# Splitting every transfer of rows on 125 partitions into one of 112 and one of 13 partitions

## The reference

```
x = x + graph_0(layernorm(x), edges, types64)   # attention of each edge's source, softmax by destination
x = x + experts_0(layernorm(x))                 # 2 of 8 experts per node
x = x + graph_1(layernorm(x), edges, types6)    # sums by relation, attention over 6 relations
x = x + experts_1(layernorm(x))                 # 2 of 8 experts, hidden size 1024
x = x + graph_2(layernorm(x), degree**-0.5)     # normalised neighbour sums, then a product
x = x + experts_2(layernorm(x))                 # dense over 8 experts
x = x + graph_3(layernorm(x), edges)            # neighbour sums
x = x + experts_3(layernorm(x))                 # shared and 4 gated experts
```

## Time and profile before

| | us |
|---|---|
| median of 3 runs | 4976.39 (4974.26 to 4980.61) |
| profiled execution, its time | 4979.84 |
| profiled execution, its span | 4977.6 |
| PE busy / DVE busy / ACT busy / POOL busy | 84% / 53% / 31% / 37% of the span |
| queue of SP's transfers: packets, MB | 405810, 490.95 |

### The profile page before, as it was taken

One profiled execution on the slowest core, in us unless ns is written; L12 is line 12 of the kernel. 1 busy time (PEld: TensorE's weight loads), 2 busy tenths in 40 slices (PEclk: granted clock), 3 DMA queues, 4 the chain that ended last, 5 costly groups with the idle time before them and its releaser, 6 DMA issues. The chain is left out here.

```text
span 4977.6 us, 70703 instructions
## 1 busy us (share of the span) xinstructions
PE 4160.5 (84%) x21605; PEld 3198.6 (64%) x21605; DVE 2661.7 (53%) x5828; ACT 1549.6 (31%) x3042; POOL 1840.2 (37%) x1628
## 2 busy tenths in 40 slices
PE   4899995864917999889999668997799999979978
PEld 2565653643715666568888657886687767768855
DVE  4588888888138999836665560002433322233354
ACT  0233331011314333345565324443001333310023
POOL 0477773872446767536666402113100000000011
PEclk9899997986968999999999879998899999999989
DMA  1599994830845666647666419996423000022200
GB/s 66 177 286 287 295 281 141 260 98 26 264 145 166 181 181 182 190 149 204 184 180 170 138 44 338 323 323 189 122 74 88 1 1 1 2 82 77 61 14 26
DMA packets 519774, 748.78 MB, mean 150 GB/s; under 512 B 80123, under 2 KB 438273, under 8 KB 519301
## 3 DMA queue, kind: packets, MB, share of 16 engines
q1 hardware_dynamic: 405810, 490.95, 31.9%
q0 software_dynamic: 62656, 189.33, 13.8%
q10 hardware_dynamic: 50960, 64.09, 3.7%
HBM read 526.98 MB, written 217.19 MB: 150 GB/s over the span
## 5 line engine op out<-in xcount | busy, mean ns | idle before, releaser
L2828 PE MATMUL sum_ps<-table_rows,block_weights 128*125 128x256 f32 x2500 | 564.7, 386 | 37.1 <-DMA table_rows<-k_table 37.1
L2828 PEld LDWEIGHTS sum_ps<-table_rows,block_weights 128*125 128x125 f32 x2500 | 465.6, 189 | 136.2 <-issue 70.2
L109 POOL DMA_INDIRECT rows_all<-kv_table,src_of_visit x416 | 445.1, 1070 | 221.6 <-issue 111.8
L2632 POOL TENSOR_TENSOR window_sums<-window_sums,brought_blocks 128x650 f32<-128x650 f32 x320 | 427.8, 1337 | 223.6 <-ACT running_blocks L2642 140.2
L2521 POOL DMA_INDIRECT gathered_rows<-k_table,src_of_chunk x392 | 409.2, 1044 | 208.4 <-issue 113.9
L2743 PE MATMUL sum_ps<-gathered_rows,hit 128*126 x1376 | 364.6, 390 | 22.6 <-DVE window_sums L2709 19.0
L2810 DVE TENSOR_TENSOR block_weights<-raw 128x625 f32<-128x625 uint16 x248 | 183.6, 805 | 349.7 <-PE sum_ps L2828 323.6
L2570 PE MATMUL block_ps<-cell_hot,low_hot 128*128 128x325 bf16 x1280 | 231.8, 304 | 141.5 <-DVE cell_hot L2560 140.4
L2057 DVE TENSOR_TENSOR y<-out_ps,b 128x256 f32<-128x256 f32 x120 | 51.0, 425 | 553.0 <-PE out_ps L1956 553.0
L3327 POOL MEMSET eps<- 125x1 f32 x1 | 0.1, 98 | 917.8 <-POOLq L2770 917.8
L2579 ACT ACTIVATE block_copies<-block_ps 128x650 bf16<-128x650 f32 x320 | 227.9, 712 | 358.1 <-PE block_ps L2570 356.7
(11 more groups left out here) (500 smaller groups left out, 8245.8 us busy)
## 6 DMA issues: line engine op xcount, KB each, us to landing
w<-in_L_ffn_W SPq DMA_DIRECT2D x112, 1024.0 KB, 7.5
v_kept<-rows_all SPq DMA_DIRECT2D x104, 512.0 KB, 5.0
v_rows<-v_kept SPq DMA_DIRECT2D x104, 512.0 KB, 4.5
visit_blocks<-block_copies ACTq DMA_DIRECT2D x320, 162.5 KB, 2.9
brought_blocks<-visit_blocks SPq DMA_DIRECT2D x320, 162.5 KB, 3.3
blocks<-running_blocks SPq DMA_DIRECT2D x320, 162.5 KB, 3.5
raw<-blocks SPq DMA_DIRECT2D x250, 162.5 KB, 2.2
w<-in_L_ffn_w SPq DMA_DIRECT2D x64, 256.0 KB, 3.7
```

The lines of the kernel that those rows point to most:

```text
L109: pool.indirect_dma_start(env.ring[:, k % KEPT_RING, i, :], None, env.kv_table, bass.IndirectOffsetOnAxis(env.src_of_visit[:, k * VB + i:k ...
L2632: pool.tensor_tensor(self.totals[:, k % 2, :], self.totals[:, (k - 1) % 2, :], self.brought[:, k % self.BROUGHT, :], ALU.add).then_inc(sel ...
L2828: mm = pe.matmul(sum_ps[0:P, t % banks, 0:D], weights[0:k, t % floats, h, :], rows[0:k, h, :], start=h == 0, stop=h == BH - 1)
```

## The change

Two constants are added: `HALVES = ((0, 112), (112, P))` and `BOTH = 16 * len(HALVES)`. At each of the eleven places where rows on 125 partitions are loaded or stored, the one transfer becomes a loop over `HALVES` with two transfers of the same bytes, one of partitions 0 to 111 and one of partitions 112 to 124, both on the same semaphore, and every wait that counted 16 for such a transfer counts 32. Broadcast loads on 125 partitions (biases, `gamma`, `beta`) stay as they are, and so do all transfers on 128 partitions. The diff, cut to its kinds:

```diff
+HALVES = ((0, 112), (112, P))
+BOTH = 16 * len(HALVES)
...
-                sp.dma_start(env.x[:], a["x"].rearrange("(t p) d -> p t d", p=P)).then_inc(x_landed, 16)
+                for lo, hi in HALVES:
+                    sp.dma_start(env.x[lo:hi], a["x"].rearrange("(t p) d -> p t d", p=P)[lo:hi]).then_inc(x_landed, 16)
...
-                sp.wait_ge(x_landed, 16)
+                sp.wait_ge(x_landed, BOTH)
...
-                    sp.dma_start(env.kv_table[g * GN:(g + 1) * GN, :].rearrange("(t p) d -> p t d", p=P),
-                                 kv_rows[:, half * GT:(half + 1) * GT, :]).then_inc(kv_stored[half], 16)
+                    for lo, hi in HALVES:
+                        sp.dma_start(env.kv_table[g * GN:(g + 1) * GN, :].rearrange("(t p) d -> p t d", p=P)[lo:hi],
+                                     kv_rows[lo:hi, half * GT:(half + 1) * GT, :]).then_inc(kv_stored[half], 16)
...
-                    pool.wait_ge(kv_stored[half], 16 * len(range(half, G, 2)))
+                    pool.wait_ge(kv_stored[half], BOTH * len(range(half, G, 2)))
...
-                        v.wait_ge(kv_stored[g % 2], 16 * (g // 2))
+                        v.wait_ge(kv_stored[g % 2], BOTH * (g // 2))
...
-                        sp.dma_start(env.rows[:, g * GT:(g + 1) * GT, :], env.kv_table[g * GN:(g + 1) * GN, D:2 * D].rearrange(
-                            "(t p) d -> p t d", p=P)).then_inc(own_landed, 16)
-                sp.wait_ge(own_landed, 16 * G)
+                        for lo, hi in HALVES:
+                            sp.dma_start(env.rows[lo:hi, g * GT:(g + 1) * GT, :], env.kv_table[g * GN:(g + 1) * GN, D:2 * D].rearrange(
+                                "(t p) d -> p t d", p=P)[lo:hi]).then_inc(own_landed, 16)
+                sp.wait_ge(own_landed, BOTH * G)
...
-                    sp.dma_start(env.x[:, ts, :], env.x_kept[:, ts, :]).then_inc(x_landed[g], 16)
-                    sp.dma_start(o_rows[:, ts, :], rows_of(env.o_table, g)).then_inc(o_landed[g], 16)
+                    for lo, hi in HALVES:
+                        sp.dma_start(env.x[lo:hi, ts, :], env.x_kept[lo:hi, ts, :]).then_inc(x_landed[g], 16)
+                    for lo, hi in HALVES:
+                        sp.dma_start(o_rows[lo:hi, ts, :], rows_of(env.o_table, g)[lo:hi]).then_inc(o_landed[g], 16)
...
-                        sp.dma_start(env.x_kept[:, g * GT:(g + 1) * GT, :], env.x[:, g * GT:(g + 1) * GT, :]).then_inc(moved, 16)
+                        for lo, hi in HALVES:
+                            sp.dma_start(env.x_kept[lo:hi, g * GT:(g + 1) * GT, :], env.x[lo:hi, g * GT:(g + 1) * GT, :]).then_inc(moved, 16)
...
-                    sp.dma_start(rows_of(env.k_table, g), next_rows[:, half * GT:(half + 1) * GT, :]).then_inc(rows_stored[half], 16)
+                    for lo, hi in HALVES:
+                        sp.dma_start(rows_of(env.k_table, g)[lo:hi], next_rows[lo:hi, half * GT:(half + 1) * GT, :]).then_inc(rows_stored[half], 16)
```

More of the change, by code:

```diff
@@ L519, in _ @@
                     sp.wait_ge(kv_made, (g + 1) * GT)
-                    sp.dma_start(env.kv_table[g * GN:(g + 1) * GN, :].rearrange("(t p) d -> p t d", p=P),
-                                 kv_rows[:, half * GT:(half + 1) * GT, :]).then_inc(kv_stored[half], 16)
+                    for lo, hi in HALVES:
+                        sp.dma_start(env.kv_table[g * GN:(g + 1) * GN, :].rearrange("(t p) d -> p t d", p=P)[lo:hi],
+                                     kv_rows[lo:hi, half * GT:(half + 1) * GT, :]).then_inc(kv_stored[half], 16)
                 for half in range(2):
-                    sp.wait_ge(kv_stored[half], 16 * len(range(half, G, 2)))
+                    sp.wait_ge(kv_stored[half], BOTH * len(range(half, G, 2)))
             @block.gpsimd
@@ L1398, in _ @@
                     sp.wait_ge(normed, (g + 1) * GT)
-                    sp.dma_start(env.token_table[g * GN:(g + 1) * GN, :].rearrange("(t p) d -> p t d", p=P),
-                                 env.rows[:, g * GT:(g + 1) * GT, :]).then_inc(tokens_stored, 16)
-                sp.wait_ge(tokens_stored, 16 * G)
+                    for lo, hi in HALVES:
+                        sp.dma_start(env.token_table[g * GN:(g + 1) * GN, :].rearrange("(t p) d -> p t d", p=P)[lo:hi],
+                                     env.rows[lo:hi, g * GT:(g + 1) * GT, :]).then_inc(tokens_stored, 16)
+                sp.wait_ge(tokens_stored, BOTH * G)
             @block.gpsimd
@@ L1632, in _ @@
                     sp.wait_ge(rows_made, (g + 1) * GT)
-                    sp.dma_start(rows_of(env.token_table, g), env.rows[:, g * GT:(g + 1) * GT, :]).then_inc(tokens_stored, 16)
-                sp.wait_ge(tokens_stored, 16 * G)
+                    for lo, hi in HALVES:
+                        sp.dma_start(rows_of(env.token_table, g)[lo:hi], env.rows[lo:hi, g * GT:(g + 1) * GT, :]).then_inc(tokens_stored, 16)
+                sp.wait_ge(tokens_stored, BOTH * G)
             @block.gpsimd
@@ L1646, in start @@
                 def start(g):
-                    v.wait_ge(x_landed[g], 16)
+                    v.wait_ge(x_landed[g], BOTH)
                     for t in group(g):
@@ L1691, in turn @@
                     if t % GT == 0:
-                        pe.wait_ge(o_landed[t // GT], 16)
+                        pe.wait_ge(o_landed[t // GT], BOTH)
                     if t >= 2:
@@ L1894, in _ @@
                         sp.wait_ge(x_made, (g + 1) * GT)
-                        sp.dma_start(env.x_kept[:, g * GT:(g + 1) * GT, :], env.x[:, g * GT:(g + 1) * GT, :]).then_inc(moved, 16)
+                        for lo, hi in HALVES:
+                            sp.dma_start(env.x_kept[lo:hi, g * GT:(g + 1) * GT, :], env.x[lo:hi, g * GT:(g + 1) * GT, :]).then_inc(moved, 16)
                     sp.wait_ge(rows_ready, (g + 1) * GT)
                     half = g % 2
-                    sp.dma_start(rows_of(env.k_table, g), next_rows[:, half * GT:(half + 1) * GT, :]).then_inc(rows_stored[half], 16)
+                    for lo, hi in HALVES:
+                        sp.dma_start(rows_of(env.k_table, g)[lo:hi], next_rows[lo:hi, half * GT:(half + 1) * GT, :]).then_inc(rows_stored[half], 16)
                 for half in range(2):
-                    sp.wait_ge(rows_stored[half], 16 * len(range(half, G, 2)))
+                    sp.wait_ge(rows_stored[half], BOTH * len(range(half, G, 2)))
                 if kind == "L0":
-                    sp.wait_ge(moved, 16 * G)
+                    sp.wait_ge(moved, BOTH * G)
             @block.gpsimd
@@ L2032, in finish @@
                             if t % GT == 0 and g >= 2:
-                                act.wait_ge(rows_stored[g % 2], 16 * (g // 2))
+                                act.wait_ge(rows_stored[g % 2], BOTH * (g // 2))
                             act.activation(next_rows[:, at, :], normed[:, at, :], ACT.Identity, bias=env.ones[0:P, 0:1]).then_inc(rows_ready, 1)
@@ L2063, in scale @@
                     if t % GT == 0 and t >= 2 * GT:
-                        v.wait_ge(rows_stored[t // GT % 2], 16 * (t // GT // 2))
+                        v.wait_ge(rows_stored[t // GT % 2], BOTH * (t // GT // 2))
                     v.wait_ge(projected, t + 1)
@@ L2174, in _ @@
                     sp.wait_ge(rows_ready, (g + 1) * GT)
-                    sp.dma_start(env.k_table[g * GN:(g + 1) * GN, :].rearrange("(t p) d -> p t d", p=P),
-                                 env.node_sums[:, g * GT:(g + 1) * GT, :]).then_inc(stored, 16)
-                sp.wait_ge(stored, 16 * G)
+                    for lo, hi in HALVES:
+                        sp.dma_start(env.k_table[g * GN:(g + 1) * GN, :].rearrange("(t p) d -> p t d", p=P)[lo:hi],
+                                     env.node_sums[lo:hi, g * GT:(g + 1) * GT, :]).then_inc(stored, 16)
+                sp.wait_ge(stored, BOTH * G)
             @block.gpsimd
@@ L3320, in _ @@
                     sp.wait_ge(biased, (g + 1) * GT)
-                    sp.dma_start(env.out[g * GN:(g + 1) * GN, :].rearrange("(t p) d -> p t d", p=P),
-                                 env.x[:, g * GT:(g + 1) * GT, :]).then_inc(stored, 16)
-                sp.wait_ge(stored, 16 * G)
+                    for lo, hi in HALVES:
+                        sp.dma_start(env.out[g * GN:(g + 1) * GN, :].rearrange("(t p) d -> p t d", p=P)[lo:hi],
+                                     env.x[lo:hi, g * GT:(g + 1) * GT, :]).then_inc(stored, 16)
+                sp.wait_ge(stored, BOTH * G)
             @block.gpsimd
```

## The result

The changed kernel takes 4928.6 us (median of 4 runs, 4916.21 to 4937.31) against 4975.33 for the kernel before (the three runs above and a fourth): a ratio of 0.9903, interval 0.9879 to 0.9927. The forecast was 4923, from 4904 to 4945. The profiled execution took 4937.31 us, with a span of 4935.5: it is the slowest of the four, and 42.1 us shorter in span than the one before.

What follows compares the result with a forecast made beforehand. No engine was taken to bound the whole; only exposed transfers on five DMA engines count. Terms of 6.5, 19, 10, 8 and 9.6 sum to 53.1 us, taking the median 4976.39 to 4923.3, range 4904 to 4945.

Steps and rivals of the forecast that it cites:

- The mechanism: Transfers on 125 partitions: five engines work; parts of 112 and 13 use 16 and 13, gaining 3.2 us per exposed transfer.
- The first rival: Attend phase becomes DMA-bound, half of its 19 us or less comes: 4934 us; chance 0.12.
- no spreading: Rival: both parts run on the same few engines, or partition count isn't the cause; nothing gained, 4979 us; chance 0.04.
- a slower pair: Rival: second part on one engine, first on five; 7.4 us in place of 5.2 per transfer, 5009 us; chance 0.03.
- The fourth rival: More than the upper bound: gathers beside the stores at the ends of the experts' phases gain too, 4905 us; chance 0.04.
- Keys and values: Last store before the next phase: wait of 10.4 us becomes 3.6, gain 6.5 us with the issue, bounds 5 and 7.
- Attend phase: Five group loads no longer starve POOL of `v_rows`: gain 19 us, bounds 10 and 22.
- the ring: Attend phase: eight batches (16 us of work) stand ahead, against a lateness of 0.5 us a load.
- Layer 0's experts, end: Three stores in line, 15.7 us become 5.5: gain 10 us, bounds 8 and 13.
- Relation router's start: Two group loads ahead of six small tensors clear sooner: gain 8 us, bounds 6 and 10.
- Three ends: `k_table` after layer 1's experts, `k_table` of the wide tail, and the result: 3.2 us each, 9.6 us, bounds 7.5 and 10.5.
- At nothing: the load of x: Setup: the load of x is behind DVE's tables and SP waits for those, so no change in time.

Runs made afterwards that it cites:

- e2: The changed kernel with the boundary at 96, parts of 96 and 29 partitions: 5041.97 us, ratio 1.0125 to the kernel before.
- e3: The changed kernel with the boundary at 115, parts of 115 and 10 partitions: 4983.58 us, ratio 1.0009 to the kernel before.
- e7: The changed kernel with the boundary at 60, parts of 60 and 65 partitions: 4948.66 us, ratio 0.9923 to the kernel before.
- e5: The changed kernel run again unaltered, for a second series and a second profile: 4924.45 us, ratio 0.9889 to the kernel before.
- e4: The kernel before with the split (112 and 13) in the attend phase's five loads alone: 4958.9 us, ratio 0.9954.
- e9: The changed kernel with the setup's edge lists in parts (96 and one), plus the relation router's two broadcasts in parts of 112 and 13: 4912.25 us, run once.
- e10: As e9, with the relation router's six small tensors issued ahead of the loads of group 0: 4900.33 us, ratio 0.9825.
- e1: The changed kernel with x in the setup loaded whole by one transfer on 125 partitions: 4934.82 us, ratio 0.9903.

## Why the prediction was right, and where it was off

**The mechanism held.** Five engines became 16, and e2 and e3 show that it is the division and not the number of transfers that does it. e7 shows that the number of engines is not all: their rate can change with it. The first rival (the attend phase DMA-bound) didn't come: the share is 0.98 from 836 to 905 us, so the engines are full, but PE loses nothing. That is where the forecast had it, 8.6 us of transfers against 8.1 of work with a ring to cover the rest; there is no room beyond that: in e7, at 293 GB/s, PE is busy only 66.42 of the same 69 us. The rivals of no spreading and of a slower pair did not happen here. e3 was built to give the first of them (4983.58 against 4979) and e2 comes near the second, with 7.3 us on the busiest engine against 7.4 (5041.97 against 5009). The fourth rival, 4905, didn't come either.

**Keys and values**: forecast 6.5 us, the stage is 5.2 us shorter (5.5 in e5). Within its bounds, a little less by the slower engines (20 GB/s in place of 22.5) and by the pair of issues (0.83 us).

**Attend phase**: forecast 19, measured 21.9 in the profile and 21.4 in e4. That is all of what was lost there; that the ring took the 0.5 us a load fits with it.

**Layer 0's experts, end**: forecast 10. From SP's last store to POOL's first gather it was 16.62 us (1476.51 to 1493.13) and is 6.66 (1457.51 to 1464.17): 10.0. The whole stage is 11.3 and 12.4 us shorter.

**Relation router's start**: forecast 8 with bounds 6 and 10, measured 5.5 (22.21 to 16.75). This term was mis-sized, and outside its bounds. I took 22.5 GB/s an engine from the loads of `table_rows`, and the group loads don't reach it. With nothing but group loads issued, first in the kernel before and then in the changed one:

```profile
2840.00:2860.00 20.00, 19.61 (x133) 17.92 (x132) 12.46 (x30) 7.37 (x23) 9.99 (x14) 0.89 0.33 120
...
2806.00:2809.00 3.00, 3.00 (x24) 2.81 (x24) 1.75 (x3) 1.13 (x4) 2.66 (x4) 1.00 1.09 231
```

Five engines moved 120 GB/s, 24 each; sixteen move 231, 14.4 each. At 14.4 GB/s the 81,920 bytes of the two group loads take 5.7 us in place of 3.6 (an estimate), 2.1 of the 2.5 us that are missing. By e9 and e10 it was neither the broadcasts nor the order, and in e10 the small tensors seem to be through before the groups' data starts. What an engine's time the small pieces (8, 32 bytes) take beside the groups, where the share is 1.19 at 262 GB/s, is not shown, and why the group loads are slower than those of `table_rows` is open.

**Three ends**: SP's waits fell by 3.5 or 3.6 us each, less some 0.6 for the longer pair of issues: 3.0 us against 3.2. In the program's end 7.39 us (from the issue to the span's end) became 4.41. The stages of those ends vary by more than this (527.2 to 534.7 us), so the line shows it and the table doesn't.

**The setup**: forecast nothing, measured 3.8 us lost (3.0 of it by e1). The step that failed is "At nothing: the load of x". I asked when x itself is needed, and not what else is in flight when it runs on all engines. The last edge list runs on one engine. DVE had it at 36.63 beside x on five engines and at 39.56 beside x on sixteen. In that stretch the engines moved 245 GB/s at a share of 1.07, some 15 GB/s each; in the kernel before it was 119 at 0.33, 22.5 each:

```profile
30.00:36.00 6.00, 0.00 (x0) 0.00 (x0) 0.00 (x0) 0.00 (x0) 0.00 (x0) 1.00 0.33 119
```

So each engine is slower while all sixteen carry x, and the list that moves beside it lands 2.93 us later. Whether x was on the list's engine before the change already, no view shows.

**The sum**: 5.2 + 21.9 + 11.3 + 5.5 + 9.0 - 3.8 = 49.1 us. The medians differ by 46.7 and 54.2 us in the two series, the profiled spans by 42.1. The score phase, 5.7 us longer in that profile and not tied to the change, brings the sum to 43.4, near the 42.1 of the spans. That the forecast of 4923 comes so near 4928.6 and 4924.45 is in part luck: against its terms the attend phase and the experts brought 4.2 us more, and keys and values, the router, the three ends and the setup 8.2 us less.

## What to carry to other kernels

Read the share of the DMA engines in a stretch in which one transfer stands alone: 0.32 of 16 says that five work, and splitting the count so that the larger part divides over 16 frees the others. A transfer on a prime count (97 here, one engine) was worth most: 30 us of the setup in the trace, 22 in the medians. Two transfers for one gain nothing otherwise and can lose: price the stage as a rate (bytes on the busiest engine against the work of a group), not the last transfer alone, and ask of each transfer that is spread wider what else is in flight beside it, since each engine may then be slower.

## What the runs showed of the hardware that was not expected

- Sixteen engines do not move 16/5 of five: 20 GB/s each (316 at a share of 1.00) against 24.6 (123 at 0.32) for the store of keys and values, and 15 GB/s each (245 at 1.07) against 23 (119 at 0.33, in the same window of the kernel before) for the load of x, and 14 each (231 at 1.09) against 24 (120 at 0.33) for the group loads of the relation router. The loads of `table_rows` on 128 partitions reach 22.5 each on sixteen; what makes the difference is open.
- With parts of 60 and 65 the rate was lower still in places: 194 GB/s at 0.87 for 3 us of the store of keys and values, 14 an engine (then 20 again), and 171 at 1.06 for the load of x, 11 an engine. This is one profile.
- A pair of issues holds SP 0.83 us where one transfer took 0.25. But where two loads of 625 KB on five engines stood ahead, the next issue took 6.57 us, and with the same bytes on sixteen engines 0.40.
- The score phase, which holds none of the changed transfers, took 616 to 632 us in twelve profiles of eleven kernels; this alone is 0.3% of the kernel's time.
